# h0's row blocks fetched by indirect transfers from GpSimd instead of two-block transfers from SyncE

## What is computed

```python
# layer 0
a  = adj * (y @ y.T)
a  = a / max(sum(|a|, axis=1), 1e-12)
x  = layernorm(x + 0.9 * (a @ x) + 0.1 * h0)
# layer 1
filt    = tanh(adj * adj) * (adj > 0);  keep the 350 largest of each row
h2      = tanh(x @ W_proj + b_proj)
feat    = relu(filt_kept @ (h2 @ W_gcn) + b_gcn)
x  = layernorm(x + feat)
```

## Time and profile before

| | us |
|---|---|
| median of 3 runs (lowest, highest) | 468.42 (467.56, 468.70) |
| span of the profiled execution | 465.9 |
| what lies around the span, by the median | 2.5 |

### The profile page before, as it was taken

One profiled execution on the slowest core, in us unless ns is written; L12 is line 12 of the kernel. 1 busy time (PEld: TensorE's weight loads), 2 busy tenths in 40 slices (PEclk: granted clock), 3 DMA queues, 4 the chain that ended last, 5 costly groups with the idle time before them and its releaser, 6 DMA issues.

```text
span 465.9 us, 15131 instructions
## 1 busy us (share of the span) xinstructions
PE 438.7 (94%) x5104; PEld 386.3 (83%) x5104; DVE 377.9 (81%) x1359; ACT 263.5 (57%) x355; POOL 161.5 (35%) x310
## 2 busy tenths in 40 slices
PE   3659999999999999999999999999999999999994
PEld 2448898888888988888888887888888888888883
DVE  5988999999999999999999976675575575575562
ACT  4997998999999999999999934900000000000000
POOL 3022543455444455554445541221211211211222
PEclk9977999999999999999999999999999999999998
DMA  8999999999999999999999200000000000000000
GB/s 262 411 414 420 419 417 417 415 408 411 409 422 420 422 423 420 424 423 412 417 419 422 60 2 1 13 11 17 17 11 17 17 11 17 17 11 17 17 11 23
DMA packets 25518, 108.50 MB, mean 233 GB/s; under 512 B 5097, under 2 KB 15490, under 8 KB 15490
## 3 DMA queue, kind: packets, MB, share of 16 engines
q1 hardware_dynamic: 25490, 108.14, 57.5%
HBM read 105.57 MB, written 2.56 MB: 232 GB/s over the span
## 4 chain that ended last, share of the span: by engine, by line
PE 75%; DVE 10%; ACT 5%; issue 5%; DMA 2%; POOL 2%; POOLq 0%; DVEq 0%; ACTq 0%; SPq 0%
PE acc L521 64%; PE words L471 6%; DVE a_bits L783 3%; DMA a_rows<-in_adj_dram 2%; PE feat_acc L584 2%; PE proj_acc L595 2%; ACT count_out L685 2%; DVE turned L870 2%; PE xnt_acc L576 1%; ACT count_out L678 1%; ACT x_parts L664 1%; POOL xs L438 1%; ACT count_out L754 1%; DVE z_high L921 1%; ACT count_out L746 1%
## 5 line engine op out<-in xcount | busy, mean ns | idle before, releaser
L521 PE MATMUL acc<-x_parts,turned 128*128 128x257 f16 (+1 forms) x1600 | 195.2, 276 | 3.2 <-DVE turned L870 1.0
L678 ACT ACTIVATE count_out<-a_rows,ones 128x2688 bf16<-128x2688 f32 (+1 forms) x80 | 190.2, 2377 | 0.5 <-DMA a_rows<-in_adj_dram 0.2
L521 PEld LDWEIGHTS acc<-x_parts,turned 128*128 128x128 fp8e4 (+1 forms) x1600 | 154.4, 98 | 28.9 <-issue 3.8
L521 PE MATMUL acc<-f_parts,turned 128*128 128x256 f16 (+1 forms) x1560 | 171.6, 273 | 0.8 <-DVE turned L870 0.8
L521 PEld LDWEIGHTS acc<-f_parts,turned 128*128 128x128 fp8e4 (+1 forms) x1560 | 152.0, 98 | 19.3 <-issue 1.3
L783 DVE TENSOR_SCALAR a_bits<-a_rows 128x2688 bf16<-128x2688 f32 (+1 forms) x80 | 116.7, 1459 | 2.7 <-DMA a_rows<-in_adj_dram 2.3
L421 POOL TENSOR_TENSOR var_eps<-mean_var,consts 128x1 f32<-128x1 f32 x80 | 18.6, 232 | 266.1 <-DVE mean_var L1077 139.7
L870 DVE TENSOR_SCALAR turned<-a_words 128x320 uint16 (+1 forms) x305 | 66.9, 233 | 53.2 <-PE acc L521 52.8
L424 POOL TENSOR_TENSOR rstd<-var_eps,consts 128x1 f32<-128x1 f32 x80 | 86.5, 1081 | 6.3
L870 DVE TENSOR_SCALAR turned<-same_class 128x320 uint16<-128x320 uint16 x313 | 71.3, 254 | 0.1
L471 PEld LDWEIGHTS words<-pack,a_bits 128*128 128x128 bf16 (+1 forms) x1600 | 51.3, 97 | 9.7 <-DVE a_bits L783 7.8
(11 more groups left out here) (111 smaller groups left out, 288.3 us busy)
## 6 DMA issues: line engine op xcount, KB each, us to landing
a_rows<-in_adj_dram SPq DMA_DIRECT2D x39, 1344.0 KB, 7.8
a_rows<-in_adj_dram SPq DMA_DIRECT2D x39, 1156.0 KB, 8.3
out_dram<-xn SPq DMA_DIRECT2D x39, 64.0 KB, 1.5
h_rows<-in_L_gnn_h_dram SPq DMA_DIRECT2D x19, 128.0 KB, 8.1
xs<-in_x_dram SPq DMA_DIRECT2D x3, 640.0 KB, 10.0
xs<-in_x_dram SPq DMA_DIRECT2D x1, 512.0 KB, 10.3
y_nat<-in_L_gnn_y_dram SPq DMA_DIRECT2D x1, 304.0 KB, 3.6
a_rows<-in_adj_dram SPq DMA_DIRECT2D x1, 84.0 KB
```

Source lines behind the costliest of these rows:

```text
L521: mm = pe.matmul(acc[par][0:m, 0:cols], bits, parts[:, b, 0:cols], start=first and b == blocks[0], stop=last and b == blocks[-1])
L678: act.activation(count_out[0:m, 0:w], a_rows[par][h][0:m, 0:w], ACT.Relu, bias=ones[0:m, 0:1], scale=-HUGE, accum_out=col).then_inc(s_coun ...
```

## The change

h0's rows no longer come by SyncE. GpSimd makes a table of row numbers (`row_index`, one column a block, by three `iota` instructions at its start) and issues, at the head of each of its steps t = 0 to 39, one indirect transfer for block t: 128 rows of 512 B, each fetched by its number in the table. There are four single buffers instead of two paired ones, each with a semaphore; a load waits until `h0_part` of block n-4 is made. GpSimd's loop over four steps is gone: its 47 steps are written out one after the other. SyncE's loop goes over two steps and has only adj in it.

```diff
-        h0_rows = [sb(f"h0_rows{p}", [P, 2, F]) for p in range(2)]
+        h0_rows = [sb(f"h0_rows{p}", [P, F]) for p in range(4)]
+        row_index = sb("row_index", [P, NB], U32)
...
             load_rows(1, 1, 0)
-            load_h0(0, 0, 0, 0, 0)
-            load_h0(1, 1, 0, 0, 1)
             sp.dma_start(wp[:, :], w_proj).then_inc(s_in["wp"], 16)
...
-            def step(t, par, pair, i, c):
+            def step(t, par, pair):
                 if not isinstance(t, int) or t >= 2:
                     load_rows(t, par, pair)
-                if valid(t - 1) and c >= 4 and par == 0:
-                    load_h0(t - 1, 1, pair - 1, i, c - 1)
-            steps4(sp, step, 4, 5)
+            steps(sp, step, 0)
...
+            pool.iota(row_index[:, 0:1], pattern=[[0, 1]], base=0, channel_multiplier=1).then_inc(s_index, 1)
+            pool.iota(row_index[:, 1:FULL], pattern=[[2 * P, (FULL - 1) // 2], [1, 2]], base=P, channel_multiplier=2)\
+                .then_inc(s_index, 1)
+            pool.iota(row_index[:, FULL:NB], pattern=[[0, 1]], base=FULL * P, channel_multiplier=1).then_inc(s_index, 1)
+            pool.wait_ge(s_index, 3)
+
+            def load_h0(n):
+                m = rows_of(n)
+                if n >= 4:
+                    pool.wait_ge(s_h0part, n - 3)
+                pool.indirect_dma_start(h0_rows[n % 4][0:m, :], None, h0,
+                                        bass.IndirectOffsetOnAxis(ap=row_index[0:m, n:n + 1], axis=0)).then_inc(s_h0[n % 4], 16)
+
+            def residual(n, par):
                 m = rows_of(n)
-                slot, turn = h0_group(i, c)
-                pool.wait_ge(s_h0[slot], turn * 16 + 16)
+                pool.wait_ge(s_h0[n % 4], n // 4 * 16 + 16)
                 pool.wait_ge(s_xh, n)
-                pool.tensor_tensor(h0_part[0:m, :], h0_rows[slot][0:m, h0_place(c), :],
+                pool.tensor_tensor(h0_part[0:m, :], h0_rows[n % 4][0:m, :],
...
-            def step(t, par, pair, i, c):
+            def step(t, par):
                 odd = (par + 1) % 2
+                if valid(t):
+                    load_h0(t)
                 if valid(t - 2):
-                    residual(t - 2, par, i, c - 2)
+                    residual(t - 2, par)
...
-            steps4(pool, step, LAG, LAG + 2)
+            for t in range(NB + LAG):
+                step(t, t % 2)
```

More of the change, by code:

```diff
@@ L24 @@
 U16 = mybir.dt.uint16
+U32 = mybir.dt.uint32
 F8 = mybir.dt.float8e4
@@ L108, in steps @@
             step(t, t % 2, t // 2)
[L110 to L127, removed]
     def valid(b):
@@ L250, in packed_path @@
         s_rows = [[sem(f"s_rows{p}{h}") for h in range(2)] for p in range(2)]
-        s_h0 = [sem(f"s_h0{p}") for p in range(2)]
+        s_h0 = [sem(f"s_h0{p}") for p in range(4)]
+        s_index = sem("s_index")
         s_bits = sem("s_bits")
@@ L334, in load_rows @@
                                  rows_in(adj, t, par, pair, HALF[h])).then_inc(s_rows[par][h], 16)
[L336 to L347, removed]
             sp.dma_start(pair_view(y_nat, 1, FULL), pairs_of(y, 1, FULL)).then_inc(s_in["y"], 16)
@@ L402, in _ @@
                                base=0, pattern=[[-1, P]], channel_multiplier=1).then_inc(s_const, 1)
-            def residual(n, par, i, c):
-                m = rows_of(n)
-                slot, turn = h0_group(i, c)
-                pool.wait_ge(s_h0[slot], turn * 16 + 16)
+            pool.iota(row_index[:, 0:1], pattern=[[0, 1]], base=0, channel_multiplier=1).then_inc(s_index, 1)
[4 more added lines that the diff above has]
+            def load_h0(n):
+                m = rows_of(n)
+                if n >= 4:
[5 more added lines that the diff above has]
+                pool.wait_ge(s_h0[n % 4], n // 4 * 16 + 16)
                 pool.wait_ge(s_xh, n)
-                pool.tensor_tensor(h0_part[0:m, :], h0_rows[slot][0:m, h0_place(c), :],
+                pool.tensor_tensor(h0_part[0:m, :], h0_rows[n % 4][0:m, :],
                                    alpha[0:m, :].to_broadcast([m, F]), ALU.mult).then_inc(s_h0part, 1)
                 pool.wait_ge(s_h0part, n + 1)
-                if not isinstance(n, int) or n >= 2:
+                if n >= 2:
                     pool.wait_ge(s_z, n - 1)
```

## The result

The kernel after takes 472.02 us (median of 3 runs, 470.87 to 472.61) against 468.42 before: ratio 1.008, 95% interval 1.0055 to 1.0104. A second measurement gave 1.0079 (1.0060 to 1.0097). It is slower, as predicted, but by 3.6 us where 22 were predicted. The profiled span is 470.8 us against 465.9.

A forecast was written before the change was run, and what follows sets the result against it. VectorE, nearly without slack beside full TensorE and DMA in phase one, was taken to pay added time. Span 465.9 + 22.3 = 488.2 us, plus 2.5 around it = 490.7, given as 490.5; range 467 to 506.

The forecast's parts named there:

- The bound: Phase one: TensorE, VectorE and DMA full; VectorE has 0.08 us slack in a 6.23 us step, so added time is paid.
- The hold, 36 x 0.62 = 22.3 us: Full stretch: each of loads 4 to 39 makes VectorE's `xn` or `turned` late by 0.62 us; chance 0.50.
- The written-out loops: GpSimd's steps: writing the loops out frees it of register work it has time for; nothing.
- The start: Adj's transfers in the start: block 2 up to 0.46 us earlier, but h0's first loads beside it; 0, bounds ±0.5 us.
- Iotas, landing, SyncE's transfers: Iotas ahead of a 20.46 us wait, loads landing with 12.5 us of room, SyncE's two-block transfers gone: nothing each.
- Half-size pieces: DMA: twice as many pieces of half the size; taken as 0, bounds 0 and +5.8 us.
- Hidden: Rival: descriptors do not hold VectorE and GpSimd spends idle time; 468.4 us, give or take 1.4; chance 0.25.
- GpSimd late: Rival: `var_eps` comes after VectorE's next cast has begun, `xn` 0.53 us late; 19 us, 487.5 us; chance 0.06.
- DMA pays: Rival: half-size pieces cost DMA up to +5.8 us, 474 us; chance 0.10.

The follow-up runs named there:

- the step by pairs: Kernel after with 21 indirect loads in place of 40, blocks 1 to 38 by pairs with 128 row numbers of 1 KB: 469.47 us, ratio 1.0018.
- the second run of after: Kernel after measured once more, unchanged, against the kernel before: 471.53 us, ratio 1.0079.

## Why the prediction was wrong in size

*The bound.* Right that VectorE time added to a step is paid: 0.166 us added to it made the step 0.147 longer. But VectorE time taken away is not given back in full: with plain transfers it fell by 0.130 us a step from before and the step by 0.024, as VectorE waited for adj. Steps of 6.85 us, TensorE at 0.9 and DMA under 390 GB/s, which I named as signs, did not show.

*The hold, 36 x 0.62 = 22.3 us.* This is the term that failed: 0.62 us of VectorE's time a step, where the loads of after add 0.05. It was wrong on two counts. The issue was longer than I took (1.06 us, not 0.72), but VectorE is free for its first half; in each step shown, only what is due in the last 0.5 to 0.6 us is held, for 0.2 to 0.4 us. And I added the hold to the step as it stood, though the load also pushes `h_part` and `xh` to where `z_high` and `z` run, which take no longer for it. The old holds, 0.43 us in the step by pairs, go, and the new one comes. Measured: the step is 0.06 to 0.10 us longer than without loads, and 36 loads cost 3.0 to 3.9 us in all; where the load stands so that no hold is saved, the step is 0.135 to 0.147 longer, or about 5 us over 36. The Trainium skill, SBUF — State Buffer, Who interferes with whom, describes the lock as one for the whole instruction; for an indirect load the trace does not agree, as `xn` and a `turned` ran at 0.34 and 0.23 us in its first half.

*The written-out loops, taken as nothing.* Wrong by the two measurements of that change alone: -0.03 us a step, 0.3% or 1.2 to 1.4 us. It hides about a third to a half of the loads' price, which is why the steps of before and after look equal (6.245 and 6.238). Why GpSimd's loop costs VectorE anything was not tested.

*The end, taken as nothing.* It was no step of mine at all: 1.4 us of DRAIN. That the change came out slower beyond the noise owes much to it: the loads less the loop's gain are 1.6 to 2.7 us, and the DRAIN brings them to 3.0 to 4.1, against 3.6 measured. The right sign was in part luck.

*The start, 0 within 0.5 us.* What a single execution shows there (0.1 to 1.3 us) isn't repeatable enough to refute or confirm it.

*Iotas, landing, SyncE's transfers.* Right as far as seen: DMA moved 420 GB/s against 413, and the wait for h0 appears once, 1.7 us, in the start.

*Half-size pieces, taken as 0.* Not quite: in 100 to 260 us VectorE waited for adj for 0.7 us in the second run of after, 1.1 with loads 0 to 3 early and 2.7 with plain transfers, and not at all before or without the loads. The first profile of after names no such wait there. That is 0.03 to 0.04 us a step with indirect loads where it shows, and 0.11 with plain transfers. Whether the size of the pieces does it or GpSimd's queue beside SyncE's is not shown.

*The stretch of 60 to 75 us.* Between blocks 5 and 8, eight of the nine profiles with indirect loads there lost 0.6 to 1.2 us (the one with every load twice 0.2), the ones with plain transfers, with SyncE's or with none at most 0.1. Part of it is seen: a check of y's, `holds` at 70.86 us, takes 0.66 us over a load's end (0.34 before). The rest is not settled.

*The rivals.* "Hidden" (468.4) fits the unchanged step, but by luck: the loads do hold VectorE, and the written-out loop and the old holds that go offset it. It also lacked the end. "GpSimd late" needs a second load. "DMA pays" (474) has a time close to the measured one, but most of that time has other causes: the DRAIN, and VectorE's own longer work. A part of it is true: the second run of after has 0.05 us a step of added idle time, with a wait for adj in it, and with plain transfers of the same half-size pieces the waits for adj are what keeps the step at 6.221.

## What to carry to other kernels

Before a hold between two engines is added to a step, lay the new instruction into the timeline and see which of the old holds it pushes away; only the difference counts. Where an instruction stands in the step can then matter more than its length: the same load cost 0.06 to 0.10 us ahead of `h_part` and 0.15 between `h_part` and `xh`. Where other resources are as full, work taken off the first is not won in full: a step with 0.13 us less of VectorE's time was only 0.02 us shorter. And read the last lines of the program: work that is hidden everywhere can come back in the closing DRAIN.

## What the runs showed of the hardware

GpSimd's closing DRAIN grows with the number of transfers that GpSimd has issued: 0.055 to 0.184 us with none, 0.151 with one, 0.555 with 4, 1.787 with 21, 3.342 with 40, 6.282 with 76. Between 4 and 21 that is 0.072 us each, between the last three 0.082 ((6.282 - 3.342) / 36 and (3.342 - 1.787) / 19), whether indirect or plain, of 64 or 128 KB, and though the last one had landed some 200 us before. Here the others' end covers the first 2.0 us of it (467.2 to 469.2), by estimate some 23 transfers: (2.0 - 0.07) / 0.082.

In the full stretch an indirect load of 128 rows takes GpSimd 1.06 us with rows of 512 B and 1.07 with 1 KB; a plain transfer of 64 KB takes 0.62. A load that begins when a long cast of VectorE's is running ends 0.8 to 0.9 us after the cast: at 152.12 after one that ends at 151.31, in 2.07 us, with every load twice.
